# A graph network's tile loops put at the first slot of a fetch block, with a shorter loop on GpSimd

## The chip, the cores and the metric

The kernel runs on one core of one Trainium2 chip. The metric is the device time of one execution in microseconds: the median of the runs shown. Engines are named as the profile names them: PE is TensorE, DVE is VectorE, ACT is ScalarE, POOL is GpSimd, SP is SyncE; a q behind the name (DVEq) is the engine's sequencer, which executes register, branch and semaphore instructions.

## The reference, cut to what matters

A graph of 3125 nodes and 103125 edges (each node has a loop to itself), 16 relations, 128 features, 4 heads, 3 layers. Each layer gathers, for every node, the rows of its edges, sums the messages and makes an attention average over the same edges:

```python
for l in range(L):                                    # L = 3
    ht = jnp.einsum('nd,rdo->nro', h, W_rel[l])       # a row per node and relation
    h_rel = jax.ops.segment_sum(ht[src, etype], dst, num_segments=n) + h @ W_loop[l] + b_rel[l]
    z = (h @ W_gat[l]).reshape(n, H, DH)
    el, er = jnp.sum(z * attn_l[l], -1), jnp.sum(z * attn_r[l], -1)
    e = jax.nn.leaky_relu(el[src] + er[dst], 0.2)
    ex = jnp.exp(e - jax.ops.segment_max(e, dst, num_segments=n)[dst])
    alpha = ex / jax.ops.segment_sum(ex, dst, num_segments=n)[dst]
    h_gat = segment_sum(alpha[:, :, None] * z[src], dst).reshape(n, D) + b_gat[l]
    hc = jnp.concatenate([h_rel, h_gat], axis=1) @ W_fuse + b_fuse
    if l == 0: hc = hc * sigmoid(concatenate([hc, avg], 1) @ W_gate + b_gate)
    h = jax.nn.relu(hc)
return _layernorm(x + h)
```

## The kernel before

**Layout.** A table in HBM holds, for each node and relation, a row of 260 numbers: the message of that relation (128), z with the logit of each head between (132). There are two tables, used in turn by the layers. The nodes are ranked by degree and cut into T = 25 tiles of 128. A tile has as many slots as its largest degree; slot k of a tile is one indirect DMA of GpSimd that fetches 128 rows, one for each node (helper `fetch`, line 609). The indices are columns of the array `ell`, 80 a tile.

**Groups.** The slots of a tile are taken in groups of 16, each into its own buffer: H (the first 16), M1, M2, then M1 again for slots 49 to 64, and the tail T of up to 15. A tile of over 64 + 15 slots fetches further blocks of indices (hub code, lines 636 to 675 and 719 to 727). The indices of the groups are first copied by VectorE into small arrays of their own: `stage_head` and `stage_mid` a tile ahead, `stage_tail` at the start of the tile itself (line 1318).

**Order of the work.** Each engine has its own loop over the 25 tiles, written out once for each of the three layers, and they meet only at semaphores:
- GpSimd (lines 699 to 742) gathers H, M1, M2, the tail, and then stores the rows of the tile before (line 688; in the last layer the output, line 694). The tail is gathered by nested Ifs over the bits 8, 4, 2, 1 of the slot count (lines 617 to 626), which write out every combination. A buffer is filled again when VectorE has summed it (`free`, line 603). The tail waits for `stage_tail`.
- VectorE (lines 1423 to 1462) clears the tail buffer (line 1315), stages the tail's indices (1318), and for each group makes logits (1328 to 1338), sums messages (1346), multiplies by the exponentials (1352) and sums the weighted z (1356). Then it divides (1370 to 1375), and in the last layer normalises (1396 to 1418).
- ScalarE (lines 862 to 881) makes the exponentials of each group (829), and after them, in the same order of its instructions, the fused node values and the copies of the next layer's table rows from PSUM, in four chunks (line 755).
- TensorE (lines 1074 to 1084) transposes, multiplies by the fuse and gate weights, and makes the table rows in four chunks (line 900). In the last layer there is no table.

The slot count of a tile is read by each engine at the start of its iteration (`load_slots`; its register instructions carry lines 351 and 354), and the end of an iteration has the line of the loop statement (741 on GpSimd, 1461 on VectorE).

Of the kernel before, what the change touches and what calls it, by code (L numbers as in the profile page):

```python
# [7 lines left out]
AX = mybir.AxisListType  # L8
F32 = mybir.dt.float32
# [4 lines left out]
P = 128  # L14
PAIR = 16
BLOCK = 64
ELL = BLOCK + PAIR
# [6 lines left out]
def gnn_kernel(nc, x, src, dst, etype, eweight, W_rel, b_rel, W_loop, W_gat, attn_l, attn_r, b_gat,  # L24
# [34 lines left out]
    with ExitStack() as ctx:  # L59
# [120 lines left out]

        GROUPS = dict(H=16, M1=16, M2=16, T=15)
# [15 lines left out]
        stage_mid = sb("stage_mid", [P, BLOCK - PAIR], U32)  # L197
# [151 lines left out]
        def load_slots(eng, t):  # L349

            n = eng.value_load(tile_slots[0:1, bass.ds(t, 1)], min_val=PAIR, max_val=E)  # L351
            pairs = counter(eng, f"pairs_{nc.next_id()}", 0)
            in_first = counter(eng, f"in_first_{nc.next_id()}", 0)
            eng.reg_alu(pairs, n, PAIR.bit_length() - 1, ALU.logical_shift_right)
            eng.reg_alu(in_first, pairs, BLOCK // PAIR, ALU.min)
            return n, eng.snap(pairs, min_val=1, max_val=E // PAIR), eng.snap(in_first, min_val=1, max_val=BLOCK // PAIR)

        def bits(eng, n, mask):

            some = counter(eng, f"some_{nc.next_id()}", 0)  # L360
            eng.reg_alu(some, n, mask, ALU.bitwise_and)
            return eng.snap(some, min_val=0, max_val=mask)

        def hub_blocks(eng, pairs):
# [4 lines left out]
            eng.reg_sub(left, pairs, BLOCK // PAIR)  # L369
            eng.reg_sub(blocks, pairs, 1)  # L370
# [7 lines left out]
            return eng.snap(blocks, min_val=1, max_val=E // BLOCK), groups_of_block  # L378
# [99 lines left out]
        def _(pool):  # L478
# [149 lines left out]
            def hub_indices(stage, K):  # L628
                pool.reg_add(at_now, at, 0)
                here = pool.snap(at_now, min_val=0, max_val=(HUB + 1) * ELL - K)  # L630
                g.tensor_copy(stage.bitcast(I32), ell_flat[:, bass.ds(here, K)]).then_inc(s_staged, 1)
                pool.reg_add(at, at, K)
                pool.wait_ge(s_staged, n_staged)
                pool.reg_add(n_staged, n_staged, 1)

            def next_block(t, first):
# [5 lines left out]
                with pool.If(first):  # L642
                    g.tensor_copy(blk_start[:], meta[:, bass.ds(t, 1), M_START]).then_inc(s_blk, 1)
                    done()
                    g.tensor_copy(blk_left[:], meta[:, bass.ds(t, 1), M_CNT]).then_inc(s_blk, 1)
                    done()
# [52 lines left out]
            def tile(l, t):  # L699
# [18 lines left out]
                with pool.If(pairs > BLOCK // PAIR):  # L718
                    blocks, groups_of_block = hub_blocks(pool, pairs)
                    with pool.Fori(0, blocks) as b:  # L720
                        next_block(t, b < 1)
                        pool.reg_mov(at, HUB * ELL)
                        with pool.Fori(0, groups_of_block()):
                            free("M2")
                            hub_indices(stage_hub[:], PAIR)
                            gather(l, "M2", stage_hub)
                    hub_indices(stage_tail[:], PAIR - 1)
                with pool.If(bits(pool, n, PAIR - 1) > 0):
                    free("T")
                    gather_tail(l, n, PAIR // 2)  # L730
# [3 lines left out]
            for l in range(L):  # L734
# [6 lines left out]
                with pool.Fori(0, T) as t:  # L741
                    tile(l, t)
# [5 lines left out]
        def _(act):  # L748
# [339 lines left out]
        def _(dve):  # L1088
# [185 lines left out]
            v.tensor_copy(stage_mid[:].bitcast(I32), ell[:, 0, PAIR:BLOCK]).then_inc(s_mid, 1)  # L1274
# [24 lines left out]
            n_tail = counter(dve, "v_tail_staged", 1)  # L1299
            n_stored = counter(dve, "v_stored", 16)  # L1300
# [6 lines left out]
            def stage_next_mid(t):  # L1307
                dve.wait_ge(s_mid, n_mid)
                dve.reg_add(n_mid, n_mid, 1)
                v.tensor_copy(stage_mid[:].bitcast(I32), ell_flat[:, bass.ds((t + 1) * ELL + PAIR, BLOCK - PAIR)]  # L1310
                              ).then_inc(s_mid, 1)

            def stage_this_tail(t, in_first):
# [3 lines left out]
                at = dve.snap(in_first * PAIR + t * ELL, min_val=0, max_val=(T + 1) * ELL - PAIR)  # L1317
                v.tensor_copy(stage_tail[:].bitcast(I32), ell_flat[:, bass.ds(at, PAIR - 1)]).then_inc(s_tail, 1)  # L1318
# [104 lines left out]
            def tile(l, t):  # L1423
                n, pairs, in_first = load_slots(dve, t)
                stage_this_tail(t, in_first)
# [6 lines left out]
                with dve.If(in_first > 3):  # L1432
                    group("M1")
                with dve.If(pairs > BLOCK // PAIR):
                    blocks, groups_of_block = hub_blocks(dve, pairs)
                    dve.reg_mov(lower_by, 16 * PAIR)
                    with dve.Fori(0, blocks):
# [5 lines left out]
                        with dve.Fori(0, groups_of_block()):  # L1443
                            group("M2")
                stage_next_mid(t)
                in_tail = bits(dve, n, PAIR - 1)
                with dve.If(in_tail > 0):
# [9 lines left out]
            for l in range(L):  # L1457
# [3 lines left out]
                with dve.Fori(0, T) as t:  # L1461
# [23 lines left out]
```

## Time and profile before

| | us |
|---|---|
| median of 3 runs | 4204.2 |
| the runs | 4196.84, 4204.68, 4204.2 |
| the profiled execution, whole | 4196.33 |
| its span, first to last instruction | 4194.8 |
| GpSimd busy | 2524.9 |
| VectorE busy | 2589.9 |
| ScalarE busy | 458.4 |
| TensorE busy | 713.2 |

The profiled execution's own time is 1.5 us above its span, and 7.9 below the median of the runs. Busy time counts neither the sequencers' instructions nor waits. In the rows, `[6.93 <-issue]` is idle time of the engine before the instruction and what ended it; "issue" is time in which it waited for nothing that the trace shows, "remote" an update whose author the trace doesn't name.

### The profile page before, as it was taken

How to read it: one execution, taken by the hardware profiler on the slowest of the kernel's cores; microseconds unless marked ns; L12 is line 12 of the kernel's file. 1: busy time of each engine (PE TensorE's matmuls, PEld its weight loads, DVE VectorE, ACT ScalarE, POOL GpSimd, SP SyncE). 2: the span in 40 equal slices, each digit the busy share in tenths (PEclk: the TensorE clock that was granted, in tenths of full speed). 3: DMA queues.
4: the chain of work that ended last, by engine and by line, in shares of the span. 5: the costliest groups of instructions: out<-in, count | busy, mean ns of one | idle time of the engine just before them, and what ended most of it. 6: DMA issues, size and time to landing. Idle time of an engine off the chain costs nothing. (4 is left out here: it accounts for less than half of the span.)

```text
span 4194.8 us, 18977 instructions
## 1 busy us (share of the span) xinstructions
PE 713.2 (17%) x1896; PEld 354.9 (8%) x1896; DVE 2589.9 (62%) x3225; ACT 458.4 (11%) x944; POOL 2524.9 (60%) x2681
## 2 busy tenths in 40 slices
PE   7630121121221220111111121220000000000000
PEld 5310000000100110000000000110000000000000
DVE  6325666666656564766666656564567776665666
ACT  4330111011111110111111111110000000000000
POOL 0257666555666646766666766646666655566563
PEclk9865555555555555555555555555555555555555
DMA  5765444433444444444444444444333333233232
GB/s 214 266 242 126 136 115 124 121 120 119 132 126 150 131 126 115 140 131 131 131 130 126 138 130 153 130 124 113 84 96 91 86 82 81 76 90 87 78 88 54
DMA packets 153682, 517.15 MB, mean 123 GB/s; under 512 B 47272, under 2 KB 54648, under 8 KB 140864
## 3 DMA queue, kind: packets, MB, share of 16 engines
q0 software_dynamic: 132384, 452.73, 37.6%
q1 hardware_dynamic: 21280, 64.25, 4.1%
q14 instruction: 15, 0.12, 0.0%
q8 instruction: 3, 0.05, 0.0%
HBM read 351.66 MB, written 165.18 MB: 123 GB/s over the span
## 5 line engine op out<-in xcount | busy, mean ns | idle before, releaser
L609 POOL DMA_INDIRECT meta_nat<-table,stage_head x1200 | 1137.4, 948 | 711.7 <-issue 563.0
L609 POOL DMA_INDIRECT late<-table,stage_mid x768 | 726.6, 946 | 234.0 <-issue 231.2
L609 POOL DMA_INDIRECT scratch<-table,stage_tail x558 | 527.5, 945 | 314.8 <-issue 314.5
L1042 PE MATMUL ps_mix<-ident,hr 128*128 128x128 f32 x75 | 35.7, 475 | 3167.2 <-DVE hg L1375 1662.6
L900 PE MATMUL ps_tab<-wrel,hT 128*128 128x512 f32 x600 | 402.3, 802 | 124.5 <-issue 106.2
L1352 DVE TENSOR_TENSOR meta_nat<-meta_nat,ps_cnt 128x2112 f32<-128x2112 f32 x75 | 176.3, 2350 | 366.4 <-issue 272.7
L1356 DVE TENSOR_REDUCE acc<-meta_nat 128x132 f32<-128x2112 f32 x75 | 290.3, 3871 | 7.7
L1042 PEld LDWEIGHTS ps_mix<-ident,hr 128*128 128x128 f32 x75 | 13.7, 182 | 3231.4 <-DVE hg L1375 1701.9
L1346 DVE TENSOR_REDUCE acc<-meta_nat 128x128 f32<-128x2048 f32 x75 | 281.9, 3759 | 0.0
L1315 DVE MEMSET scratch<- 128x1920 f32 x75 | 124.3, 1658 | 241.6 <-issue 241.6
L1356 DVE TENSOR_REDUCE acc<-scratch 128x132 f32<-128x2112 f32 x69 | 266.5, 3862 | 7.1
L1346 DVE TENSOR_REDUCE acc<-scratch 128x128 f32<-128x2048 f32 x69 | 258.7, 3750 | 10.7 <-issue 2.1
L829 ACT ACTIVATE ps_cnt<-logit 128x68 f32<-128x68 f32 x192 | 44.4, 231 | 1968.5 <-issue 1049.1
L755 ACT ACTIVATE rows<-ps_tab 128x512 f32<-128x512 f32 x300 | 176.7, 599 | 612.5 <-remote 450.5
L1328 DVE TENSOR_TENSOR raw<-meta_nat,er_cur 128x64 f32<-128x64 f32 x75 | 20.0, 267 | 296.6 <-DMA meta_nat<-table,stage_head 228.6
L1356 DVE TENSOR_REDUCE acc<-late 128x132 f32<-128x2244 f32 x48 | 195.5, 4072 | 5.0
L1346 DVE TENSOR_REDUCE acc<-late 128x128 f32<-128x2176 f32 x48 | 189.7, 3952 | 8.9 <-remote 2.7
L900 PEld LDWEIGHTS ps_tab<-wrel,hT 128*128 128x128 f32 x600 | 142.2, 259 | 317.7 <-issue 253.2
L1352 DVE TENSOR_TENSOR scratch<-scratch,ps_cnt 128x2112 f32<-128x2112 f32 x69 | 161.7, 2343 | 0.0
L688 POOL DMA_INDIRECT table<-rows,stage_id x50 | 48.8, 976 | 142.7 <-ACT meta L763 127.8
L834 ACT ACTIVATE hrT<-ps_mix,brel 128x128 f32<-128x128 f32 x75 | 27.5, 367 | 883.8 <-issue 474.9
L1352 DVE TENSOR_TENSOR late<-late,ps_cnt 128x2244 f32<-128x2244 f32 x48 | 119.0, 2480 | 0.0
(189 smaller groups left out, 1516.4 us busy)
## 6 DMA issues: line engine op xcount, KB each, us to landing
table<-rows SPq DMA_DIRECT2D x50, 1040.0 KB
meta_nat<-table,stage_head POOLq DMA_INDIRECT x1200
late<-table,stage_mid POOLq DMA_INDIRECT x768
scratch<-table,stage_tail POOLq DMA_INDIRECT x558
meta<-meta_ranked POOLq DMA_DIRECT2D x1, 3250.0 KB
xin<-in_x SPq DMA_DIRECT2D x48, 64.0 KB, 4.4
table<-rows,stage_id POOLq DMA_INDIRECT x50
late<-in_dst SPq DMA_DIRECT2D x1, 402.8 KB
```

The costliest lines, as they stand in the source:

```text
L609: pool.indirect_dma_start(out=slots[b][:, k, :], out_offset=None, in_=table[l % 2], in_offset=bass.IndirectOffsetOnAxis(ap=index, axis=0)) ...
L688: pool.indirect_dma_start(out=table[(l + 1) % 2][0:NP_ * R, :].rearrange("(n r) f -> n (r f)", r=R), out_offset=bass.IndirectOffsetOnAxis( ...
L755: s.activation(rows[k][:, c * RC:(c + 1) * RC, 0:D], ps_tab[c % 2][:].rearrange("p (r f) -> p r f", r=RC), ACT.Copy).then_inc(s_bank[(c + ...
L829: s.activation(wgt[:, :, :, 0], logit[:], ACT.Exp).then_inc(s_wgt, 1)
L834: s.activation(hrT[:], mix[0], ACT.Identity, bias=brel[:, l:l + 1])
L900: pe.matmul(ps_tab[c % 2][:], hT[k][:], wrel[:, l, c * RC * D:(c + 1) * RC * D], start=True, stop=True).then_inc(s_chunk[c], 1)
L1042: pe.transpose(mix[0], hr[:], ident[:])
L1315: v.memset(messages("T", 1, PAIR), 0.0)
L1328: v.tensor_tensor(raw[:, 1:K + 1], logits_of(b, 1, K + 1), er_cur[:].to_broadcast([P, K, H]), ALU.add).then_inc(s_raw, 1)
L1346: v.tensor_reduce(acc[:, 0:D], messages(b, lo, K + 1).rearrange("p k d -> p d k"), AX.X, ALU.add).then_inc(s_part, 1)
L1352: v.tensor_tensor(weighted(b, lo, K + 1), weighted(b, lo, K + 1), wgt[:, lo:K + 1].to_broadcast([P, K + 1 - lo, H, EX]), ALU.mult).then_in ...
L1356: v.tensor_reduce(acc[:, D:ROW], slots[b][:, lo:K + 1, D:ROW].rearrange("p k f -> p f k"), AX.X, ALU.add).then_inc(s_acc, 1)
```

## The change

The loops over tiles of GpSimd, ScalarE and VectorE are given `head_slot = 0`: the first instruction of the loop lies at the first slot of a fetch block of that engine. TensorE's and SyncE's loops stay as they are. Beside that the code of a tile is made shorter. Three groups of 16 are written out instead of four (a tile of over 48 + 15 slots goes to the hub code), a tile has 64 columns of `ell` instead of 80, and GpSimd gathers the tail by four Ifs in a row, for pieces of 8, 4, 2 and 1, each with places of its own in `stage_tail`. VectorE therefore stages the tail with four copies, each from an offset that it works out from the slot count. GpSimd's loop has 245 instructions in place of 351.

```diff
-ELL = BLOCK + PAIR
+ELL = BLOCK
+FIRST = BLOCK - PAIR
...
+        PIECES = (8, 4, 2, 1)
...
-        stage_mid = sb("stage_mid", [P, BLOCK - PAIR], U32)
+        stage_mid = sb("stage_mid", [P, FIRST - PAIR], U32)
...
-            eng.reg_alu(in_first, pairs, BLOCK // PAIR, ALU.min)
+            eng.reg_alu(in_first, pairs, FIRST // PAIR, ALU.min)
...
+        def tail_of(eng, n):
+            in_tail = counter(eng, f"in_tail_{nc.next_id()}", 0)
+            eng.reg_alu(in_tail, n, PAIR - 1, ALU.bitwise_and)
+            return in_tail
...
+        def tile_loop(eng, kind):
+            return nc.Fori(0, T, engines=[kind], head_slot={kind: 0})
...
-            def gather_tail(l, n, size, first=0):
-                with pool.If(bits(pool, n, size) > 0):
-                    for k in range(first, first + size):
-                        fetch(l, "T", 1 + k, stage_tail[:, k:k + 1])
-                    if size > 1:
-                        gather_tail(l, n, size // 2, first + size)
-                if size > 1:
-                    with pool.Else():
-                        gather_tail(l, n, size // 2, first)
+            def gather_tail(l, n):
+                first = 0
+                for size in PIECES:
+                    has = counter(pool, f"has_{nc.next_id()}", 0)
+                    pool.reg_alu(has, n, size, ALU.bitwise_and)
+                    with pool.If(pool.snap(has, min_val=0, max_val=size) > 0):
+                        for k in range(first, first + size):
+                            fetch(l, "T", 1 + k, stage_tail[:, k:k + 1])
+                    first += size
...
-                with pool.If(in_first > 3):
-                    free("M1")
-                    gather(l, "M1", stage_mid[:, 2 * PAIR:3 * PAIR])
...
-                with pool.Fori(0, T) as t:
+                with tile_loop(pool, POOL) as t:
                     tile(l, t)
...
-                with act.Fori(0, T) as t:
+                with tile_loop(act, ACTE) as t:
                     tile(l, t)
...
-                at = dve.snap(in_first * PAIR + t * ELL, min_val=0, max_val=(T + 1) * ELL - PAIR)
-                v.tensor_copy(stage_tail[:].bitcast(I32), ell_flat[:, bass.ds(at, PAIR - 1)]).then_inc(s_tail, 1)
+                first = 0
+                for size in PIECES:
+                    dve.reg_alu(piece_at, n, PAIR - 2 * size, ALU.bitwise_and)
+                    dve.reg_alu(piece_at, piece_at, dve.snap(in_first * PAIR + t * ELL), ALU.add)
+                    at = dve.snap(piece_at, min_val=0, max_val=(T + 1) * ELL - size)
+                    ins = v.tensor_copy(stage_tail[:, first:first + size].bitcast(I32), ell_flat[:, bass.ds(at, size)])
+                    first += size
+                ins.then_inc(s_tail, 1)
...
-                with dve.If(in_first > 3):
-                    group("M1")
...
-                with dve.Fori(0, T) as t:
+                with tile_loop(dve, DVE) as t:
                     tile(l, t)
```

The hub code's block arithmetic (`hub_blocks`, `next_block`) is fitted to the new limit of 48 slots, and the hub's last indices are no longer staged apart.

## Rows read from the trace of the kernel before

**Rows 1.** The page, its first line.
```profile
span 4194.8 us, 18977 instructions
```

**Rows 2.** Stretches: us, busy us (instructions) of PE, PEld, DVE, ACT, POOL; PEclk, DMA, GB/s.
```profile
381.70:1153.60 771.90, 146.09 (x253) 62.79 (x252) 501.69 (x554) 90.84 (x181) 490.93 (x518) 0.54 0.42 126
1153.60:1531.60 378.00, 89.26 (x163) 40.42 (x162) 230.32 (x280) 56.20 (x109) 245.75 (x259) 0.56 0.45 139
1677.90:2409.40 731.50, 114.78 (x225) 52.23 (x226) 494.93 (x526) 84.45 (x166) 490.53 (x518) 0.57 0.44 133
2409.40:2788.40 379.00, 75.73 (x145) 33.42 (x146) 225.88 (x262) 52.51 (x99) 248.01 (x262) 0.57 0.46 139
2953.20:3741.10 787.90, 36.84 (x112) 23.99 (x112) 540.33 (x750) 17.98 (x68) 483.12 (x510) 0.50 0.32 85
3741.10:4148.20 407.10, 23.69 (x72) 15.43 (x72) 254.17 (x405) 9.78 (x36) 249.73 (x263) 0.50 0.32 85
```

**Rows 3.** The waits, whole span: us in total, times, longest.
```profile
ACT rows L755 <- remote: 450.5, 103, 5.7
...
DVE meta_nat L1352 <- issue: 272.7, 31, 15.4
```

**Rows 4.** Timeline of VectorE, one tile of layer 0: start, us, what, idle before.
```profile
721.57 0.18 DVE L1370 RECIPROCAL rden<-acc 128x4 f32<-128x4 f32 x1
...
728.89 1.66 DVE L1315 MEMSET scratch<- 128x1920 f32 x1 [1.65 <-issue]
...
730.93 0.27 DVE L1328 TENSOR_TENSOR raw<-meta_nat,er_cur 128x64 f32<-128x64 f32 x1 [0.21 <-issue]
...
749.41 2.35 DVE L1352 TENSOR_TENSOR meta_nat<-meta_nat,ps_cnt 128x2112 f32<-128x2112 f32 x1 [13.44 <-ACT ps_cnt L829]
```

**Rows 5.** Line 755 in one tile of layer 0: ns min/median/max, first and last start.
```profile
L755 ACT ACTIVATE rows<-ps_tab x4: 592/597/597, 1335.1 to 1338.3; 128x512 f32<-128x512 f32 x4
```

**Rows 6.** Line 351, tiles 1 to 14 of layer 0, layer 2, layer 1.
```profile
L351 DVEq FUSED_REGOPS  x14: 211/211/211, 438.6 to 1152.6; - x14
...
L351 DVEq FUSED_REGOPS  x14: 211/698/710, 3028.3 to 3740.2; - x14
...
L351 POOLq FUSED_REGOPS  x14: 13/694/707, 1708.1 to 2386.6; - x14
```

**Rows 7.** Timeline of GpSimd in layer 2: two fetches, 16 apart.
```profile
3329.82 0.97 POOL L609 DMA_INDIRECT meta_nat<-table,stage_head  x1 [4.71 <-DVE acc L1356]
...
3349.87 0.95 POOL L609 DMA_INDIRECT late<-table,stage_mid  x1 [0.30 <-issue]
```

**Rows 8.** Timeline of VectorE, one tile of layer 2.
```profile
3317.71 0.27 DVE L1328 TENSOR_TENSOR raw<-meta_nat,er_cur 128x64 f32<-128x64 f32 x1 [3.33 <-issue]
...
3329.00 0.27 DVE L1328 TENSOR_TENSOR raw<-late,er_cur 128x64 f32<-128x64 f32 x1
...
3341.28 0.26 DVE L1328 TENSOR_TENSOR raw<-scratch,er_cur 128x60 f32<-128x60 f32 x1
...
3352.90 0.18 DVE L1370 RECIPROCAL rden<-acc 128x4 f32<-128x4 f32 x1
...
3369.39 1.66 DVE L1315 MEMSET scratch<- 128x1920 f32 x1 [6.93 <-issue]
```

**Rows 9.** VectorE idle in layer 2: before L1315, L1328 (tiles 1-14); before L1315 (15-24).
```profile
  issue: 93.6, 14
...
  issue: 38.8, 14
...
  issue: 31.4, 10
```

**Rows 10.** DMA queues of kind instruction: packets, MB, share of 16 engines.
```profile
q14 instruction: 15, 0.12, 0.0%
q8 instruction: 3, 0.05, 0.0%
```

**Rows 11.** Line 1318, whole span: the copy that stages the tail.
```profile
L1318 DVE COPY stage_tail<-ell x75: 132/133/326, 267.5 to 4149.9; 128x15 int32 x75
```

More of the change, by code:

```diff
@@ L8 @@
 AX = mybir.AxisListType
+POOL, ACTE, DVE = mybir.EngineType.Pool, mybir.EngineType.Activation, mybir.EngineType.DVE
 F32 = mybir.dt.float32
@@ L368, in hub_blocks @@
             now = counter(eng, f"now_{nc.next_id()}", 0)
-            eng.reg_sub(left, pairs, BLOCK // PAIR)
-            eng.reg_sub(blocks, pairs, 1)
+            eng.reg_add(left, n, PAIR - 1 - FIRST)
+            eng.reg_alu(left, left, PAIR.bit_length() - 1, ALU.logical_shift_right)
+            eng.reg_add(blocks, left, BLOCK // PAIR - 1)
             eng.reg_alu(blocks, blocks, (BLOCK // PAIR).bit_length() - 1, ALU.logical_shift_right)
@@ L376, in groups_of_block @@
                 return eng.snap(now, min_val=1, max_val=BLOCK // PAIR)
-            return eng.snap(blocks, min_val=1, max_val=E // BLOCK), groups_of_block
+            return eng.snap(blocks, min_val=1, max_val=E // BLOCK + 1), groups_of_block
+        def tile_loop(eng, kind):
+            return nc.Fori(0, T, engines=[kind], head_slot={kind: 0})
         block = ctx.enter_context(nc.Block())
@@ L645, in next_block @@
                     g.tensor_copy(blk_left[:], meta[:, bass.ds(t, 1), M_CNT]).then_inc(s_blk, 1)
+                    done()
+                    g.tensor_scalar(blk_start[:], blk_start[:], -float(PAIR), None, ALU.add).then_inc(s_blk, 1)
+                    done()
+                    g.tensor_scalar(blk_left[:], blk_left[:], float(PAIR), None, ALU.add).then_inc(s_blk, 1)
                     done()
@@ L717, in tile @@
                 pool.reg_add(n_tail, n_tail, 1)
-                with pool.If(pairs > BLOCK // PAIR):
-                    blocks, groups_of_block = hub_blocks(pool, pairs)
+                in_tail = tail_of(pool, n)
+                with pool.If(pairs > FIRST // PAIR):
+                    blocks, groups_of_block = hub_blocks(pool, n)
                     with pool.Fori(0, blocks) as b:
@@ L724, in tile @@
                             free("M2")
-                            hub_indices(stage_hub[:], PAIR)
+                            hub_indices()
                             gather(l, "M2", stage_hub)
-                    hub_indices(stage_tail[:], PAIR - 1)
-                with pool.If(bits(pool, n, PAIR - 1) > 0):
+                    pool.reg_mov(in_tail, 0)
+                with pool.If(pool.snap(in_tail, min_val=0, max_val=PAIR - 1) > 0):
                     free("T")
-                    gather_tail(l, n, PAIR // 2)
+                    gather_tail(l, n)
                 with pool.If(t > 0):
@@ L1299, in _ @@
             n_tail = counter(dve, "v_tail_staged", 1)
+            piece_at = counter(dve, "v_piece_at", 0)
             n_stored = counter(dve, "v_stored", 16)
@@ L1431, in tile @@
                     group("M2")
-                with dve.If(in_first > 3):
-                    group("M1")
-                with dve.If(pairs > BLOCK // PAIR):
-                    blocks, groups_of_block = hub_blocks(dve, pairs)
+                in_tail = tail_of(dve, n)
+                with dve.If(pairs > FIRST // PAIR):
+                    blocks, groups_of_block = hub_blocks(dve, n)
                     dve.reg_mov(lower_by, 16 * PAIR)
@@ L1444, in tile @@
                             group("M2")
+                    dve.reg_mov(in_tail, 0)
                 stage_next_mid(t)
-                in_tail = bits(dve, n, PAIR - 1)
-                with dve.If(in_tail > 0):
+                with dve.If(dve.snap(in_tail, min_val=0, max_val=PAIR - 1) > 0):
                     dve.reg_alu(tail_lands, n, PAIR - 1, ALU.bitwise_and)
```

24 lines of the change are left out of this document (10 added, 14 removed).

## The prediction, made before the change was run

> **What bounds the kernel now.** I read the stretches of the layers first, then the waits, then single tiles on each engine. The six stretches [rows 2] are, layer by layer, tiles 1 to 14 and tiles 15 to 23; they hold 3455.4 us of the profiled span of 4194.8 [rows 1]. The slots of a tile come from the degrees that the reference's inputs give (sorted, in tiles of 128): 58, 43, 41, 40, 38, 38, 37, 36, 36, 35, 34, 34, 33, 32, 32, then 31, 31, 30, 29, 28, 28, 27, 26, 24, 21: 842 a layer. Tile 0 has three full groups, tiles 1 to 14 two, the others one, and all but tiles 13 and 14 a tail. No tile reaches 64 slots, so the code for hub blocks never runs, before or after.
>
> Two paces matter. **GpSimd** starts a fetch every 1.25 us (16 of them between 3329.82 and 3349.87 [rows 7]), and a store takes the place of one more, some 1.28 us. Tiles 1 to 14 have 509 slots: 509 x 1.25 + 14 x 1.28 = 654 us. Tiles 15 to 23 have 254: 329 us. The stretches take 772, 732 and 788, and 378, 379 and 407 [rows 2], so GpSimd's fetches explain some 85 per cent of the time and something else stands in the way.
>
> What stands in the way are spells in which register instructions crawl. The same fused register operation of the slot load takes 211 ns on VectorE in all 14 tiles of layer 0's stretch, but has a median of 698 ns on VectorE in layer 2 and of 694 ns on GpSimd in layer 1 [rows 6]. One code, one engine, different places of the three copies of the loop: that looks like the supply of instructions, not like data. What it costs is seen in two places:
> - In layer 2 VectorE sits idle 6.93 us at the end of its loop [rows 8], against 1.65 in layer 0 [rows 4], and then again before the first sum of a tile: 93.6 and 38.8 us over 14 tiles [rows 9].
> - In layers 0 and 1 TensorE's semaphores for the four table chunks reach ScalarE late. ScalarE waits 4.4 us before each of 103 chunk copies (450.5 us in all), for something the trace can't name [rows 3]. Without it the four copies start within 3.2 us [rows 5]. ScalarE takes the exponentials in order behind them, so VectorE waits 13.44 us in the tile at 749.41 [rows 4], 272.7 us over 31 tiles in one row alone [rows 3].
>
> I take the second for a consequence of the first: the copies are quick exactly in tiles where I see neither VectorE nor GpSimd crawl. This is the weak step.
>
> **The change, part by part.**
> *GpSimd's loop in one block.* The nested tail code and the third inline group go, 351 instructions become 245, and the loop begins at a block's first slot, so it no longer spans blocks. The Trainium skill (Advanced Engine Details and Errata, ISA Cache) gives 256 instructions to a block and two blocks to these engines; by that 245 fit and 351 do not. VectorE's and ScalarE's loops are shorter and get the same start. If spells come from leaving a block, all three lose them.
>
> *Layers 0 and 1, tiles 1 to 14.* Without the table delay GpSimd's pace rules: 654 us each. VectorE's own pace for two groups and a tail in layer 0: head 2.04 (728.89 to 730.93), end 7.32 (721.57 to 728.89) [rows 4], groups 11.29, 12.28 and 11.62 (3317.71 to 3352.90 [rows 8]): 44.55. That is over GpSimd's 43.8, 43.8 and 42.5 for the tiles of 34, 34 and 33 slots, so add 5: layer 0 gives 659 and saves 113. Layer 1 has a shorter end, 654, and saves 77.
>
> *Layer 2, tiles 1 to 14.* VectorE: 2.04 + 35.19 + an end of 16.49 (3352.90 to 3369.39) less the 5.28 of excess idle = 48.44 a tile. Seven tiles of 37 to 33 slots take that, 339; the five of 43 to 38 take GpSimd's 200 x 1.25 + 5 x 1.28 = 256; the two of 32 take 83; near the tie some 5 more. 683, saves 105. Check from the other side: 788 less 70.5 (93.6 - 14 x 1.65) less 38.8 [rows 9] is 679.
>
> *Tiles 15 to 23.* The tail's indices are staged when VectorE starts the tile, GpSimd fetches up to 15 slots then, and VectorE waits for them: this chain is longer than GpSimd's 329. In layer 2 it now takes 407 with 31.4 of loop-end idle over ten tiles [rows 9]; less 14.9 it is 392. In layer 0 the end of a tile is 5.67 instead of 9.56 (both without the loop-end idle; [rows 4, 8]), 9 x 3.89 less: 357. In layer 1, with almost no end, GpSimd's 329 is the longer. Saved: 15, 21, 50.
>
> *What it adds.* VectorE stages the tail with four copies in place of one and about a dozen register instructions more. A copy is 133 ns [rows 11]; the register work runs ahead during the 1.66 us memset. No row shows four in a line: nothing at the low end, 3 x 0.13 + 1.0 = 1.4 us a tile at the high. I take 0.3, since copies of this size overlap and the memset covers the rest. It counts where VectorE or the tail chain decides, 29 tiles: 9 us (of which 5 stand in the sums above), at most 41. GpSimd's four Ifs in a row come while its queue holds fetches: nothing; were that cover gone, 4 x 0.25 us. ELL falls from 80 to 64 columns and the middle copy from 48 to 32: under 2 us once. Entering an aligned loop is one jump per engine and layer: nothing at best, nine times 5 us at worst (the loop-end idle above), hidden in most cases behind the wait for the first gather. I set these at 0 together. M1's third use goes with no tile that used it.
>
> **Sum.** 659 + 654 + 683 + 357 + 329 + 392 = 3074 instead of 3455.4: 381 less, and 4 for the staging. The profiled execution took 4196.3, so 3819; the median of the runs shown is 4204.2, 8 above it, and I don't carry that. Forecast 3820. Its own bounds: 3765 if the first tiles and the layer changes (the 741 us I left alone) lose their spells too, 3900 if some spells stay or the added work is at its high end.
>
> **The rivals.**
> *Only the loop ends gain (16 in 100).* TensorE isn't in the change. For it: copies are late in layer 0 even while VectorE's register instructions are quick, and what the semaphores wait for is unnamed. If TensorE's delay is its own, layer 0 stays at 772 and 378, layer 1 gains only what a table of 15 us instead of a crawling loop leaves, some 22 and 20, and layer 2 gains its 105 and 15: 4196 - 162 = 4034. Against it: the quick copies of [rows 5] run the same TensorE code. The Trainium skill (Runtime: NRT & Kernel Launch, Instruction fetch mechanics) says that sequential block crossings are mostly hidden and that a taken branch out of the two blocks held stalls for a fetch; by that rule alone loop ends gain and the rest of a tile doesn't, which is this rival. Against the rule stands that the crawl goes on for a dozen instructions after the branch.
>
> *No change (5 in 100).* The instruction queues show 15 and 3 packets in the whole run [rows 10], not one per iteration of 75. If the blocks are really held and the crawl is something else, say a limit on how fast records or semaphores drain, alignment does nothing: 4204, within 0.2 per cent (8 us, about what a measurement of this kernel can tell from no change).
>
> *Slower (7 in 100).* Same premise, but VectorE's tile start crawls as before and now holds a dozen more register instructions at 0.70 us each [rows 6]: 8 us on the path of each of layer 2's 14 first tiles and some ten of layer 1, partly under GpSimd's pace. About 100 us: 4300. It decides from three added instructions per tile that crawl and are not covered.
>
> **How the numbers follow.** The forecast holds 72 in 100 and gives 3820. Leaving out no change and slower leaves out 12; the range must reach the first rival, whose price is 4034. So 3765 to 4035. Faster is 72 + 16 = 88, same 5, slower 7.
>
> **What the profile after would show.** Right: the fused operation of the slot load at some 0.2 us in every layer on both engines; VectorE's loop-end idle near 1.65 in layer 2; ScalarE's four copies within 4 us and the wait called remote gone; VectorE's wait for the exponential near zero; GpSimd's period in layers 0 and 1 at 1.25 us a slot. Wrong in the weak step: loop ends quick, copies still 5 us apart. Wrong altogether: 0.70 us operations as before, perhaps more of them. The sum would be off if the staging of the tail came more than a microsecond later in tiles 15 to 23, which GpSimd answers one for one.

## The result and the profile after

| | us |
|---|---|
| before, median of 4 runs | 4204.4 (4196.8 to 4211.7) |
| changed, median of 4 runs | 4259.5 (4253.2 to 4260.8) |
| ratio, 95% interval | 1.0128 (1.0108 to 1.0149) |

Slower by 55 us (1.3 per cent), where 3820 and a gain were forecast. The profiled execution of the changed kernel took 4259.4:

```profile
span 4257.8 us, 19559 instructions
```

The six stretches of the changed kernel, with the columns of [rows 2]:

```profile
384.60:1163.30 778.70, 145.88 (x253) 63.00 (x252) 506.27 (x597) 90.33 (x181) 490.94 (x518) 0.54 0.41 124
1163.30:1554.40 391.10, 90.41 (x164) 39.61 (x163) 233.22 (x306) 56.40 (x109) 247.63 (x261) 0.55 0.45 135
1699.00:2445.70 746.70, 116.26 (x225) 53.15 (x225) 499.97 (x569) 84.45 (x166) 491.81 (x519) 0.56 0.43 130
2445.70:2826.40 380.70, 75.99 (x145) 34.03 (x145) 228.82 (x289) 52.51 (x99) 248.12 (x262) 0.57 0.45 139
2991.40:3801.40 810.00, 36.85 (x112) 24.00 (x112) 548.66 (x793) 17.98 (x68) 484.83 (x511) 0.50 0.31 83
3801.40:4211.10 409.70, 23.68 (x72) 15.40 (x72) 255.55 (x432) 9.78 (x36) 249.50 (x263) 0.50 0.32 84
```

They add to 3516.9 us against 3455.4 [rows 2]. Every stretch got longer, most of all tiles 1 to 14 of layer 2 (810.0 from 787.9) and of layer 1 (746.7 from 731.5). Nothing of what the prediction expected has happened: the spells (stretches in which register instructions crawl) are there in all three layers. The waits of the changed kernel (us in total, times, longest):

```profile
ACT rows L765 <- remote: 447.4, 108, 5.8
...
DVE scratch L1326 <- issue: 272.8, 75, 12.3
...
DVE meta_nat L1369 <- issue: 172.2, 22, 12.7
DVE stage_tail L1333 <- issue: 154.8, 94, 3.3
...
DVE raw L1345 <- DMA meta_nat<-table,stage_head: 133.0, 10, 36.5
DVE raw L1345 <- DMA scratch<-table,stage_tail: 126.5, 18, 11.2
...
DVE meta_nat L1369 <- ACT ps_cnt L839: 110.4, 11, 12.7
...
DVE raw L1345 <- issue: 101.1, 46, 7.8
...
DVE raw L1345 <- DMA late<-table,stage_mid: 58.8, 8, 8.9
...
DVE er_cur L1380 <- issue: 30.3, 22, 2.0
```

and, of the kernel before, the rows that answer to them and don't stand in [rows 3]:

```profile
DVE scratch L1315 <- issue: 241.6, 75, 12.1
...
DVE raw L1328 <- DMA meta_nat<-table,stage_head: 228.6, 26, 37.0
...
DVE raw L1328 <- DMA scratch<-table,stage_tail: 108.7, 18, 11.0
...
DVE meta_nat L1352 <- ACT ps_cnt L829: 93.7, 9, 13.4
...
DVE raw L1328 <- DMA late<-table,stage_mid: 82.8, 18, 8.8
...
DVE raw L1328 <- issue: 67.2, 40, 4.6
...
DVE er_cur L1363 <- issue: 13.5, 20, 1.2
```

TensorE's late chunks are as they were (447.4 us, 450.5 in [rows 3]). New is VectorE's idle time between the four staging copies, 154.8 us, and its idle before the memset, before the first operation of a group (`raw`, shown as issue) and before `er_cur` grows too (31.2, 33.9 and 16.8 us): 236.7 us more. Most of it is given back where VectorE would have waited anyway: for the exponential (172.2 + 110.4 from 272.7 + 93.7, so 83.8 less) and for fetched rows (318.3 from 420.1, 101.8 less). About 51 us of idle are left, and VectorE is busy 25.1 us longer (2615.0 from 2589.9, most of it the copies): 76 us, of the size of the 63 between the two spans (a rough account, since it holds idle time off the path too).

GpSimd is held up too. It may fetch the tail only when `stage_tail` is there. Its idle time that ended with the staging copy (us in total, times) is, in the changed kernel and then in the kernel before:

```profile
  POOL scratch L617: 220.6, 28
...
  POOL scratch L609: 127.6, 20
```

One tile of layer 2, on VectorE:

```profile
3359.34 1.66 DVE L1326 MEMSET scratch<- 128x1920 f32 x1 [6.37 <-issue]
...
3365.26 0.36 DVE L1333 COPY stage_tail<-ell 128x2 int32 x2 [1.22 <-issue]
...
3365.99 0.27 DVE L1345 TENSOR_TENSOR raw<-meta_nat,er_cur 128x64 f32<-128x64 f32 x1 [0.21 <-DVE er_cur L1380]
```

The idle time before the memset, 6.37 us, is as in [rows 8] (6.93). Then come 0.60, 1.99 and 1.22 us before copies, in which the register instructions of the offsets crawl, but the 3.33 us before the group's head in [rows 8] are down to 0.21. Together the idle time at the start of this tile is 10.4 us, from 10.3: the spell is about as long as before and the new instructions stand inside it. Eight of the 14 tiles look like this (10.3 to 10.5 us, from 9.4 to 10.2), but in three it grew to 18 to 20. The longest stand in layer 1, in four tiles in a row:

```profile
1881.08 1.66 DVE L1326 MEMSET scratch<- 128x1920 f32 x1 [9.80 <-issue]
...
1888.35 0.25 DVE L1333 COPY stage_tail<-ell 128x2 int32 x1 [2.63 <-issue]
...
1896.04 0.27 DVE L1345 TENSOR_TENSOR raw<-meta_nat,er_cur 128x64 f32<-128x64 f32 x1 [2.63 <-issue]
```

This tile has 22.1 us of idle time up to the head of its first group; in the kernel before no tile has more than 12.6. Added up over tiles 1 to 14 (waits for fetched rows left out), the idle time at the start of the tiles went from 139.7 to 175.7 us in layer 2, from 48.6 to 126.8 in layer 1 and from 25.9 to 78.2 in layer 0. The stretches themselves grew by less: 22.1, 15.2 and 6.8 us. In the whole trace 299 of VectorE's register, branch and slot-load instructions took 0.6 us or more in the kernel before, and 563 in the changed one.

In layer 0 VectorE had no spell at all in tiles 1 to 14 ([rows 6], 211 ns each time); GpSimd had them there before, too. Four of these tiles now start with 8.4 to 17.9 us of idle time, where all had 1.9 or less. The staging's own operation, whose median is 40 ns, now takes up to 1.4 us in that layer (ns min/median/max, start of the first and the last):

```profile
L1330 DVEq ALU_OP  x55: 6/40/1395, 384.6 to 1121.0; - x55
```

### The profile page after: what moved, and what is told of

The parts are those of the page before. It is cut to its first block, busy times and chain, and to the rows that moved or that the text cites. A ratio compares the mean times of both kernels' runs of the same rounds, so it can differ in the third digit from the quotient of the medians.

```text
span 4257.8 us, 19559 instructions
## 1 busy us (share of the span) xinstructions
PE 721.3 (17%) x1896; PEld 358.0 (8%) x1896; DVE 2615.0 (61%) x3450; ACT 458.7 (11%) x944; POOL 2527.3 (59%) x2681
## 4 chain that ended last, share of the span: by engine, by line
issue 45%; DVE 24%; DVEq 8%; POOL 7%; PE 5%; another core or an unknown queue 4%; DMA 2%; ACT 2%; POOLq 1%; SPq 1%; ACTq 0%; PEldq 0%
DVE acc L1373 7%; POOL scratch L617 3%; DVE scratch L1369 3%; POOL meta_nat L617 3%; DVE meta_nat L1369 3%; PE ps_tab L910 2%; DVE late L1369 2%; DVE acc L1363 2%; DVEq L1331 1%; POOL late L617 1%; DVEq L1477 1%; DVEq L1330 1%; DMA scratch<-table,stage_tail 1%; DVEq L354 1%
## 5 line engine op out<-in xcount | busy, mean ns | idle before, releaser
L1369 DVE TENSOR_TENSOR meta_nat<-meta_nat,ps_cnt 128x2112 f32<-128x2112 f32 x75 | 176.2, 2349 | 282.5 <-issue 172.2
L1326 DVE MEMSET scratch<- 128x1920 f32 x75 | 124.3, 1658 | 272.8 <-issue 272.8
L765 ACT ACTIVATE rows<-ps_tab 128x512 f32<-128x512 f32 x300 | 177.0, 599 | 616.3 <-remote 447.4
L1333 DVE COPY stage_tail<-ell 128x8 int32 (+3 forms) x300 | 34.2, 167 | 155.3 <-issue 154.8
```

The source lines that it names most:

```text
L765: s.activation(rows[k][:, c * RC:(c + 1) * RC, 0:D], ps_tab[c % 2][:].rearrange("p (r f) -> p r f", r=RC), ACT.Copy).then_inc(s_bank[(c + ...
L1326: v.memset(messages("T", 1, PAIR), 0.0)
L1369: v.tensor_tensor(weighted(b, lo, K + 1), weighted(b, lo, K + 1), wgt[:, lo:K + 1].to_broadcast([P, K + 1 - lo, H, EX]), ALU.mult).then_in ...
```

## Experiments

**The parts of the change, one by one.** The first four kernels ran beside the kernel before on one chip.

Aligned loops alone, in the kernel before:

```diff
-                with dve.Fori(0, T) as t:
+                with nc.Fori(0, T, engines=[DVE], head_slot={DVE: 0}) as t:
```

(and the same on GpSimd and ScalarE).

> The kernel before with one thing of the change: the three layers' loops on GpSimd, VectorE and ScalarE begin at the first slot of a fetch block; GpSimd's loop keeps 351 instructions. Staging theory (the four copies with their register instructions at VectorE's tile start cost the 55 us): within 10 us of before, 4204. Place theory (where the code lies decides the crawling spells): it moves, by 20 us or more, and if the start of the loops is what costs, to about 4260. My prediction's theory (leaving a block makes the spells): VectorE's spells in layer 2 go, some 50 us faster, about 4150.

The changed kernel without them:

```diff
-            return nc.Fori(0, T, engines=[kind], head_slot={kind: 0})
+            return eng.Fori(0, T)
```

> The changed kernel with plain loops, nothing of it aligned. Staging theory: about 4260, as changed. Place theory: away from 4260 by 20 us or more, towards 4204. My prediction's theory: slower than the changed kernel, since loops leave blocks again.

VectorE's four copies, with their offsets, in the kernel before:

```diff
-                v.tensor_copy(stage_tail[:].bitcast(I32), ell_flat[:, bass.ds(at, PAIR - 1)]).then_inc(s_tail, 1)
+                for size in (8, 4, 2, 1):
+                    dve.reg_alu(piece_at, n, PAIR - 2 * size, ALU.bitwise_and)
+                    dve.reg_alu(piece_at, piece_at, dve.snap(in_first * PAIR + t * ELL), ALU.add)
...
```

> The kernel before with VectorE's part of the staging alone: four copies with six register instructions more at the tile's start; GpSimd's code is that of before, so the rows that a tail's later fetches take are others than the reference's. Staging theory: the whole loss, 4250 to 4265. Place theory: 4204 or an unforeseen few us away. If both the copies and GpSimd's shorter code matter, about half, 4230.

And the changed kernel with the one copy of before in their place (the same lines the other way round):

> The changed kernel with one copy of 15 indices for the tail, at one offset, so six register instructions and three copies fewer at VectorE's tile start (the rows that the tail's pieces take are others than the reference's). Staging theory: the loss goes, 4195 to 4210, and a few us below before if GpSimd's shorter code helps. Place theory: still about 4260.

| kernel | us, median | ratio to before, 95% |
|---|---|---|
| before, beside them | 3779.8 (31 runs) | |
| aligned loops alone | 3783.3 | 1.0010 (1.0000 to 1.0020) |
| changed, plain loops | 3786.0 | 1.0015 (1.0006 to 1.0025) |
| before with four copies | 3784.2 | 1.0013 (1.0003 to 1.0022) |
| changed with one copy | 3785.2 | 1.0014 (1.0004 to 1.0023) |

(The kernel before with four copies fetches the reference's rows after all: where GpSimd reads, both stagings put the same indices. The changed kernel with one copy fetches other rows, but as many.) No theory had foreseen the first line: the very kernel that had taken 4204 took 3780, and nothing separated the others from it by more than 0.2 per cent. So both original kernels were run again.

> The changed kernel once more, beside the kernel before on the same chip, since the kernel before took 4204 us where the change was timed and 3780 us beside the last four kernels. Theory one (the spells of crawling register instructions are a condition that comes from outside the kernel, and the change lost by meeting them with more register instructions): where the kernel before takes about 3780, the changed one takes 3780 to 3795, with no spell in its trace; where the kernel before takes about 4200, the changed one takes about 4260. Theory two (alignment or the four copies cost something by themselves): 3835 beside 3780, the same 55 us.

> The kernel before once more, for its trace. Theory one: at about 3780 us its slot load's fused register operation takes some 0.2 us in every tile of every layer on VectorE and GpSimd, and ScalarE's table copies wait for no late semaphore; at about 4200 us the trace looks like the first one. Theory two makes no difference here.

Measured: changed 3789.9, before 3782.9 (19 runs) and, as a kernel of its own, 3782.4; the ratio of changed to before is 1.0018 (1.0009 to 1.0028). The 55 us had become 7. The trace of the kernel before now (span 3781.7 us), the same six stretches:

```profile
377.60:1033.10 655.50, 127.00 (x253) 61.69 (x252) 501.25 (x555) 89.40 (x181) 492.54 (x519) 0.57 0.49 148
1033.10:1391.00 357.90, 81.91 (x163) 39.60 (x162) 230.42 (x280) 56.16 (x109) 249.89 (x263) 0.58 0.50 148
1532.80:2183.80 651.00, 111.78 (x225) 52.78 (x225) 495.29 (x527) 84.39 (x166) 492.37 (x519) 0.57 0.49 149
2183.80:2514.50 330.70, 72.76 (x145) 34.28 (x146) 223.98 (x262) 52.44 (x99) 248.62 (x262) 0.59 0.53 159
2669.30:3343.70 674.40, 36.84 (x112) 24.01 (x112) 539.03 (x751) 18.01 (x68) 490.15 (x516) 0.50 0.37 101
3343.70:3735.20 391.50, 23.69 (x72) 15.43 (x72) 254.17 (x406) 9.80 (x36) 250.16 (x263) 0.50 0.33 88
```

and line 351 in tiles 1 to 14 of layer 2, where [rows 6] had a median of 698 ns on VectorE:

```profile
L351 DVEq FUSED_REGOPS  x14: 211/211/211, 2718.0 to 3342.7; - x14
```

No spell in the layers (no register, branch or slot-load instruction of VectorE or GpSimd takes 0.6 us there), and the wait called remote is gone from the list. The instruction queues show the same 15 and 3 packets as with spells [rows 10]. The changed kernel's trace of the same session, tiles 1 to 14 of layers 0 and 2:

```profile
376.22:1032.24 656.02, 125.49 (x252) 60.80 (x251) 503.82 (x597) 89.29 (x181) 491.80 (x519) 0.57 0.49 148
...
2671.72:3348.02 676.30, 36.85 (x112) 23.99 (x112) 541.52 (x792) 18.01 (x68) 489.77 (x516) 0.50 0.37 100
```

and its staging operation in layer 0, from 40 to at most 52 ns:

```profile
L1330 DVEq ALU_OP  x56: 40/40/52, 376.2 to 1031.9; - x56
```

Theory one is borne out: whether there are spells is settled outside the kernel. That left two things open: how the lost 55 us come about when the condition holds, and what brings it about.

**What late chunks and a slow staging cost.** Both can be put into a kernel by hand. Dummy copies on ScalarE hold back three of the four chunks; a dummy memset on VectorE stands ahead of three of the four staging copies; the third kernel has both.

```diff
+                    for c in range(1, 4):
+                        for r in (16, 7):
+                            s.activation(rows[1][:, 0:r], rows[1][:, 0:r], ACT.Copy).then_inc(s_idle, 1)
...
+                    if first:
+                        norm_step(v.memset(spare[:], 0.0))
```

> The kernel before with dummy copies on ScalarE that hold back the last three of a tile's four table chunks, about 5 us each, in layers 0 and 1, as the late semaphores of TensorE did in the first trace. My reading of that trace (the late chunks hold back the exponentials behind them and so set the tiles of layer 0): layer 0's tiles 1 to 14 go from 655 back to some 770, layer 1's from 651 to some 730, tiles 15 to 23 to some 378 each; layer 2 stays. 4030, at 4000 to 4070. If the spells of VectorE and GpSimd set the tiles and the late chunks lay beside them: under 3860.

> The changed kernel with a dummy clearing of some 1.8 us on VectorE ahead of each of the three later staging copies, about 5.5 us a tile, as the crawling register instructions held them in the changed kernel's first trace. If such a wait counts wherever VectorE or the tail chain sets the tile: about 50 us in layer 2's tiles 1 to 14, 45 in its tiles 15 to 23, 30 and 45 in layer 0, 30 in the rest: 3970 to 4010. If most of it is taken up elsewhere (GpSimd ahead of VectorE): under 3860.

> The changed kernel with both, late chunks and slow staging. If in layers 0 and 1 the wait for the late chunks takes the staging's delay up (VectorE starts later and then waits less for the exponential), only layer 2 adds to the kernel with late chunks alone: 95 to 110 us over it, some 4140. If they add: 200 us over it, 4240.

Measured beside a before of 3782.6: 4243.3, 4144.2 and 4422.0. Tiles 1 to 14 of layer 0 and of layer 2, late chunks:

```profile
379.17:1179.73 800.56, 143.28 (x253) 63.46 (x252) 502.70 (x554) 311.16 (x265) 490.16 (x518) 0.54 0.40 121
...
3129.64:3803.42 673.78, 36.86 (x112) 23.99 (x112) 538.98 (x751) 17.98 (x68) 489.11 (x516) 0.50 0.38 101
```

slow staging:

```profile
377.20:1088.67 711.47, 125.66 (x253) 61.11 (x252) 583.81 (x638) 89.54 (x181) 490.84 (x519) 0.56 0.45 136
...
2866.70:3627.73 761.03, 36.83 (x112) 23.98 (x112) 621.68 (x834) 17.98 (x68) 488.49 (x516) 0.50 0.33 89
```

and both:

```profile
376.24:1177.39 801.15, 143.96 (x253) 63.56 (x252) 586.59 (x638) 311.26 (x265) 491.07 (x518) 0.54 0.40 121
...
3144.65:3905.58 760.93, 36.85 (x112) 23.99 (x112) 622.20 (x834) 18.00 (x68) 490.06 (x516) 0.50 0.33 89
```

All three times lie above what was expected, because the delays were larger (the chunks came 6.1 us apart, not 5.6, and in every tile; the dummy memsets took 1.77 us each and the whole delay some 6 us) and the sums had let too many tiles off. The shares are what counts. Late chunks take layer 0 from 655.5 to 800.6 and leave layer 2 at 673.8, so by themselves they are enough to set layer 0's tiles; that they alone made the 771.9 of [rows 2], with chunks a little less late, is likely and not shown. A slow staging alone costs 55 us in layer 0 (711.5) and 85 in layer 2 (761.0). With late chunks as well it costs these tiles of layer 0 nothing (801.2 beside 800.6) and layer 2 the full amount (760.9). This is the giving back seen in the waits above: a VectorE that starts late waits less for a late exponential. Over the whole kernel the slow staging costs 354 us alone (4144.2 against the changed kernel's 3789.9 of the other session) and 179 beside late chunks (4243.3 to 4422.0, the rest of the change included).

**What brings the spells about.** First the load of register instructions: SyncE counts beside the layers.

```diff
+            with sp.Fori(0, 8000):
+                pass
```

> The kernel before with SyncE, idle from some 255 us on, counting 8000 turns of an empty loop (two register instructions a turn) behind its last transfer, which should last some 1000 us and so cover layer 0 and leave layers 1 and 2 as they are. Theory of a shared path (the spells are register instructions of several engines queueing for one outlet, which a burst fills): layer 0 shows operations of 0.70 us on VectorE or GpSimd and gets slower, by up to 120 us; layers 1 and 2 stay. Theory of an outside condition that the load of register instructions does not bring about: 3780, within 5 us, and no such operation.

Measured: 3784.2, ratio 1.0004 (0.9993 to 1.0015). SyncE issued 16,000 register and branch instructions from 263 to 2270 us, into layer 1's last tiles and twice as long as expected, and in the layers' loops none on VectorE or GpSimd took 0.6 us. Such a load on SyncE doesn't bring spells about. Next the traffic of transfers, on SyncE's queue:

```diff
+            with sp.Fori(0, 150):
+                sp.wait_ge(s_idle, n_copied)
+                sp.dma_start(spare_b[:], x[0:2048, :]).then_inc(s_idle, 16)
+                sp.reg_add(n_copied, n_copied, 16)
```

> The kernel before with 151 copies of 1 MB from DRAM to DRAM on SyncE's queue, one behind the other, from some 255 us on, beside layer 0 and part of layer 1 at least. Theory that the spells come from a crowded way to memory (register instructions that wait for their own supply or for their report behind transfers): operations of 0.70 us appear on VectorE and GpSimd while the copies run. Theory of an outside condition that this kernel's own traffic does not bring about: none appear; the fetches land later and layer 0 and 1 may take up to 100 us longer for that alone, with no register instruction over 0.3 us on VectorE.

Measured: 4175.3 beside a kernel before of 4204.6 (4 runs), ratio 0.9933 (0.9911 to 0.9956). Here the condition held again, with the kernel before alone as well, so the copies didn't make it; whether they could where there are no spells was not tried. They left the register instructions as they were (291 of VectorE's and 535 of GpSimd's took 0.6 us or more in the layers, 297 and 503 in the first trace) and took something off elsewhere: tiles 1 to 14 of layer 0 took 729.0 us, not 771.9 [rows 2], with fewer late chunks (450.5 us, 103 times, in [rows 3]):

```profile
ACT rows L764 <- remote: 355.7, 82, 5.9
```

Why fewer came late stays open.

**The parts again, with spells.** The staging alone and the change less the staging ran once more.

> The changed kernel with one copy of 15 indices at one offset (as before, some of the tail's rows are others than the reference's), sent again because some chips show the spells and others don't. On a chip with spells (kernel before 4204): if the six register instructions and three copies at VectorE's tile start are what cost 55 us there, 4195 to 4215; if it is the loops' places or GpSimd's code, about 4255. On a chip without: 3785, as it was.

> The kernel before with VectorE's four staging copies alone (GpSimd as before, so some of the tail's rows are others than the reference's). On a chip with spells: 4245 to 4270 if the staging is what costs, 4200 to 4215 if not. On a chip without: 3784, as it was.

Now the condition held, and it told the parts apart:

| kernel | us, median | ratio to before, 95% |
|---|---|---|
| before, beside them | 4206.8 (9 runs) | |
| changed with one copy | 4206.4 | 1.0000 (0.9989 to 1.0011) |
| before with four copies | 4254.0 | 1.0116 (1.0087 to 1.0145) |

Tiles 1 to 14 of layers 0 and 2, changed kernel with one copy (ScalarE's wait for late chunks is 475.4 us in all):

```profile
382.85:1158.27 775.42, 143.30 (x253) 61.56 (x252) 502.46 (x554) 91.16 (x181) 491.77 (x519) 0.54 0.44 125
...
2958.46:3752.00 793.54, 36.82 (x112) 23.95 (x112) 540.01 (x751) 17.98 (x68) 484.50 (x511) 0.50 0.34 85
```

and the kernel before with four copies (440.4 us):

```profile
381.88:1172.12 790.24, 143.51 (x255) 62.10 (x254) 505.97 (x597) 91.97 (x181) 491.22 (x519) 0.55 0.41 123
...
2987.78:3797.46 809.68, 36.82 (x112) 23.96 (x112) 548.79 (x792) 17.98 (x68) 483.20 (x510) 0.50 0.31 83
```

whose VectorE idles between the staging copies as the changed one's does:

```profile
DVE stage_tail L1323 <- issue: 128.3, 79, 3.3
```

The first is near the stretches of the kernel before (775.4 and 793.5 against 771.9 and 787.9 [rows 2]), the second at or above those of the changed one (790.2 and 809.7 against 778.7 and 810.0). VectorE's slow instructions tell the same: 262 with one copy, 532 with four (299 and 563 in the two kernels of the start), and in tiles 1 to 14 of layer 0 none and 118. So does GpSimd's idle time before the tail's fetches, 122.4 and 224.7 us. GpSimd's shorter loop and the aligned heads, the core of the change, are worth nothing measurable with spells; the staging is worth 47 of the 55 us by itself, and without it nothing is lost.

Whether it is the copies or their register instructions was not settled. Four copies at one offset were tried:

```diff
+                for size in (8, 4, 2, 1):
+                    ins = v.tensor_copy(stage_tail[:, first:first + size].bitcast(I32), ell_flat[:, bass.ds(at, size)])
```

> The kernel before with four staging copies that all read at the one offset of before, so three copies more and hardly a register instruction more (the tail's rows are others than the reference's). On a chip with spells (kernel before near 4205): if it is the register instructions that crawl, 4200 to 4215; if the number of copies costs, up to the 4254 of the kernel with four offsets. On a chip without: 3780 to 3785.

VectorE executes no register instruction more for them. They met no spells: 3781.2 beside 3778.7, ratio 1.0007 (0.9995 to 1.0018). That the register instructions crawl is seen in the trace above; that three copies without them would cost nothing with spells is argued, not shown. This run was on the chip that had shown spells for the two kernels before it.

**A version that beats both where there are no spells.** There the prediction's other chain is in plain sight: in tiles 15 to 23 of layers 0 and 2 VectorE clears and stages the tail only when it starts the tile, and GpSimd and VectorE then wait for each other. The staging can come a tile earlier, behind the sums, where VectorE waits for TensorE and ScalarE:

```diff
                 n, pairs, in_first = load_slots(dve, t)
-                stage_this_tail(t, in_first)
...
                 end_tile(t)
+                stage_this_tail(t + 1, load_slots(dve, t + 1)[2])
                 epilogue(l, t)
```

> The kernel before with the tail staged a tile ahead: VectorE clears the tail's slots and stages the next tile's indices right behind the end of a tile's sums, before the epilogue, not at the start of the next tile. Without spells the tail chain that sets tiles 15 to 23 (358 us in layer 0, 392 in layer 2, of which GpSimd and VectorE wait for each other) goes: some 25 us less in layer 0 and 50 in layer 2, and VectorE's own two-group tiles of layer 2 lose the 1.7 us clearing into the wait for the fused product: 15 us more. 3690, at 3670 to 3720, beside 3780. If the tail chain is not what sets these tiles: within 10 us of 3780. On a chip with spells both would be some 400 us longer.

(The table of slot counts gets one entry more, and tile 0's tail is staged ahead of the layers.) 3681.9 beside 3782.6, ratio 0.9734 (0.9718 to 0.9750). Tiles 15 to 23 of layers 0 and 2, from GpSimd's first fetch of one to that of the other, before (no spells) and with the move:

```profile
1012.90:1370.90 358.00, 81.60 (x162) 39.60 (x162) 231.10 (x280) 55.86 (x108) 249.91 (x264) 0.58 0.48 148
3319.50:3711.60 392.10, 23.68 (x72) 15.43 (x72) 254.85 (x406) 9.79 (x36) 250.19 (x264) 0.50 0.33 88
```

```profile
1009.10:1341.60 332.50, 81.63 (x162) 39.46 (x162) 232.95 (x284) 55.87 (x108) 249.79 (x263) 0.58 0.52 163
3277.20:3612.80 335.60, 23.70 (x72) 15.44 (x72) 257.01 (x410) 9.80 (x36) 250.29 (x263) 0.50 0.38 103
```

358.0 becomes 332.5 and 392.1 becomes 335.6, close to GpSimd's pace of 329. The same move in the changed kernel:

> The changed kernel with the same move as the kernel of 3682 us: the next tile's tail is cleared and staged behind the end of a tile's sums. If the change's 7 us without spells are the four copies and their register work at the head of VectorE's and of the tail's chain, the move hides them and the time is within 3 us of that kernel: 3680 to 3686, 0.973 to 0.975 of before. If they come from the loops' places or GpSimd's code: 3689 or more. On a chip with spells, some 400 us longer.

3679.8, ratio 0.9733 (0.9717 to 0.9749), level with the move in the kernel before: what the change cost without spells is hidden. Both ran again, to meet spells if they could.

> The changed kernel with the tail cleared and staged a tile ahead, which took 3680 on a chip without spells. On a chip with them: the register instructions are then issued behind the sums of a tile, where VectorE waits for TensorE and ScalarE anyway; if that hides them as it does without spells, 4120 to 4190 beside 4205; if the spells only move with them, 4230 or more. On a chip without: 3680, as it was.

> The kernel before with the tail staged a tile ahead, which took 3682 on a chip without spells. On a chip with them: 4080 to 4150 beside 4205 if its gain of about 100 us is kept, more than the version with four copies keeps; about 4205 or more if its second slot load a tile (five more register instructions) eats it. On a chip without: 3682, as it was.

There were none: 3678.4 (changed) and 3676.8 (before) beside 3778.7, ratios 0.9732 (0.9704 to 0.9760) and 0.9728 (0.9700 to 0.9756). How the move does with spells was not seen.

## Why the prediction was wrong

- **What bounds the kernel.** Right. Take the spells away and the six stretches become 656.0, 360.6, 651.0, 330.5, 676.3 and 393.8 us in the changed kernel, where 659, 357, 654, 329, 683 and 392 were forecast: 3068 against 3074 and 4. The whole took 3789.9 then, 30 below the forecast, since the parts that it left alone got shorter as well (some 722 us, not 741), as its lower bound allowed for. GpSimd's 1.25 us a fetch, VectorE's 48.4 us a tile in layer 2 and the tail chain are the right pieces.
- **"I take the second for a consequence of the first."** Not shown, and its reason was misread. Late chunks are enough to set layer 0's tiles (the dummy copies show it), and from session to session they and the crawl come and go together. That the crawl causes them no run showed. The copies are not "quick exactly in tiles where I see neither VectorE nor GpSimd crawl": around the quick copies of [rows 5], in tiles 15 to 23 of layer 0, GpSimd's load of the slot count takes 0.70 us in every tile (0.29 without spells), and yet five of the nine sets of four copies in that stretch start within 4.1 us:

```profile
L351 POOLq TENSOR_LOAD <-tile_slots x9: 698/700/868, 1175.8 to 1514.4; - x9
```

The other way round, the four copies from 1071 us on are spread over 12 us, and from 1030 to 1083 us neither engine has a register instruction of 0.6 us.
- **"If spells come from leaving a block, all three lose them"** is the step that failed. The changed kernel still has register instructions of 0.70 us in all three layers. With spells, aligned loops and a GpSimd loop of 245 instructions are level with the kernel before (1.0000) once the staging is taken out. Without spells, the kernel before has none with its 351 instructions and unaligned heads. So neither the place nor the length of the loops brings the spells or takes them away. I had the evidence against it in hand: 15 and 3 packets on the instruction queues [rows 10], the same without spells, in a rival that the prediction gave 5 in 100. The 381 us of the forecast hung on this step, and none of them came. The Trainium skill (Advanced Engine Details and Errata, ISA Cache), with 256 instructions to a block and two blocks, may well be right about the blocks; no run here shows a cost from them.
- **What it adds.** Without spells the whole change cost 7 us and 9 were forecast for the staging; the staging alone cost 4.4, but the change without it 5.4, so these few us can't be given to one part. With spells the rival "Slower" had it: the tile's start crawls and now holds more register instructions. It had 7 in 100 and 4300; measured were 4259. That the size came so near is partly luck, for its terms don't fit the trace. Seven instructions were added a tile, not a dozen (lines 1330 and 1331 run four times each, in place of once line 1318). They don't add 0.70 us each on top: in eight of layer 2's 14 tiles they hardly lengthen the spell, in others, above all in layer 1 and in layer 0, where VectorE had no spells, the spells grow by 6 to 20 us. And most of that is given back in later waits, for the exponential and for fetched rows.
- **"Only the loop ends gain".** Wrong too: the idle before the memset stayed, 272.8 us from 241.6. The Trainium skill (Runtime: NRT & Kernel Launch, Instruction fetch mechanics) has a stall at a taken branch whose target isn't held; no run here shows one, and without spells the same branches cost no such idle time.
- **The range** ended at 4035. All of it rested on one premise, that the change acts on the spells; the cases in which it doesn't were left out with 12 in 100. That the same kernel could run without spells was in no rival.

## What to carry to other kernels

A delay whose cause the trace can't name should not be given to the change under study: forecast both with it and without it, and look first whether the kernel has it in another session or on another chip. Register instructions at the start of a tile are cheap as long as they run ahead of data work, and cost whole microseconds where the engine crawls, so offsets are best computed where the engine waits anyway (measured here without spells alone). A step that two engines wait for in turn, here clearing and staging the tail, belongs at the end of the tile before; that was worth 2.7 per cent without spells, far more than the change ever cost or gave.

## What the runs showed of the hardware

- One program, two times: the kernel before took 4204 to 4207 us (medians) in three sessions on the chip and 3779 to 3783 in six, steady within 0.4 per cent in each. The longer one comes with register instructions of 0.70 us on VectorE and GpSimd, never on ScalarE in the kernel before, and with ScalarE's table copies 5.6 us apart, held by a semaphore. One chip showed it in one session and not in a later one, so it is not a property of the chip alone. What it is stays open. A load of register instructions on SyncE didn't bring it about (1.0004); a load of transfers ran only where it held already, and didn't end it.
- Within this condition the kernel's own code moves the spells: seven more register instructions (and three copies) at VectorE's tile start brought VectorE spells in tiles 1 to 14 of layer 0, where it had none (instructions of 0.6 us or more there: none in the kernel before and in the changed one less the staging, 107 in the changed one, 118 with the staging alone). 151 unrelated copies of 1 MB left the register instructions as they were, and made 82 table copies wait, not 103.
